# One common set of five PSUM banks for the score and max units, and q and k stored and filled by group of four heads

## The reference

```python
xn = layernorm(x)
# attention
q, k, v = heads(xn @ Wq.T), heads(xn @ Wk.T), heads(xn @ Wv.T)
q, k = rope(q), rope(k)
scores = where(causal, q @ k.T / 4, -1e9)
attn = softmax(scores) @ v
a = merge(attn) @ Wo.T
# feed-forward: a 3-tap mix along the sequence, 9 two-layer paths, one chosen per position
xm = mix(xn)
paths = (xm @ W1[p] + b1[p]) @ W2[p] + b2[p]           # p = 0..8
pick = argmax(tanh(xm @ Wo1 + bo1) @ Wo2 + bo2)
f = layernorm(xn + paths[pick]) * gamma + beta
out = x + a + f
```

## Time and profile before

| | |
|---|---|
| median of 3 runs | 783.06 us |
| the profiled execution | 784.09 us, span of its instructions 782.4 us |
| mean granted TensorE clock | 0.974 |
| PE / DVE / ACT / POOL busy | 739.9 / 641.7 / 448.9 / 288.3 us |
| in 91 to 740 us: PE / DVE / ACT busy | 639.2 / 555.0 / 389.6 of 649 us |

### The profile page before, as it was taken

How to read it: one execution, slowest core, us unless ns; L and a number is a source line. 1 busy time by engine, 2 the same in 40 slices (tenths; PEclk the granted TensorE clock), 3 DMA queues, 4 the chain that set the end, 5 groups by cost and what they waited for, 6 DMA issues and landing times.

```text
span 782.4 us, 12591 instructions
## 1 busy us (share of the span) xinstructions
PE 739.9 (95%) x4416; PEld 372.3 (48%) x4416; DVE 641.7 (82%) x1894; ACT 448.9 (57%) x780; POOL 288.3 (37%) x459
## 2 busy tenths in 40 slices
PE   4869999999999999999999999999999999999996
PEld 2432344354565544345465544445465554354544
DVE  5989999889798789888988789897988669878622
ACT  2262645765655654775656655666657555754672
POOL 2001123990615112893514213695334203130623
PEclk9965999999999999999999999999999999999999
DMA  7259050224613434112651615111560705100103
GB/s 242 97 164 191 8 114 2 72 81 113 105 15 59 105 91 77 53 60 83 118 72 28 136 56 112 33 69 53 122 109 2 136 28 112 33 2 2 28 1 81
DMA packets 40577, 59.98 MB, mean 77 GB/s; under 512 B 4813, under 2 KB 36830, under 8 KB 37634
## 3 DMA queue, kind: packets, MB, share of 16 engines
q1 hardware_dynamic: 36002, 54.39, 29.4%
q0 software_dynamic: 4224, 4.19, 4.1%
q10 hardware_dynamic: 288, 0.59, 0.2%
HBM read 42.04 MB, written 16.85 MB: 75 GB/s over the span
## 4 chain that ended last, share of the span: by engine, by line
PE 71%; POOL 10%; DVE 8%; ACT 6%; DMA 2%; issue 1%; SPq 1%; POOLq 0%; ACTq 0%; DVEq 0%
PE bank L1557 14%; PE bank L1538 14%; PE bank L1519 14%; PE bank L1500 7%; PE bank L1510 6%; PE bank L1462 3%; POOL prob L1014 3%; PE bank L1585 3%; PE bank L1473 3%; ACT prob L1132 3%; POOL raw L993 2%; POOL turned L991 2%; PE bank L1480 2%; PE bank L1567 2%; POOL turned L999 1%
## 5 line engine op out<-in xcount | busy, mean ns | idle before, releaser
L1132 ACT ACTIVATE prob<-bank 128x512 f32<-128x512 f32 x576 | 324.6, 597 | 194.4 <-PE bank L1538 191.3
L1350 DVE CUSTOM_DVE_ANT_0 bank<-bank,causal_sb 128x384 f32<-128x384 f32 (+3 forms) x512 | 240.3, 513 | 34.3 <-PE bank L1519 33.5
L1519 PE MATMUL bank<-k_st,q_st 96*128 96x512 bf16 (+3 forms) x768 | 236.1, 339 | 8.4 <-DMA q_st<-scratch 4.0
L1014 POOL TENSOR_SCALAR_AFFINE_SELECT prob<-prob 128x256 f32<-128x256 f32 (+1 forms) x320 | 125.9, 427 | 294.0 <-ACT prob L1132 291.1
L1538 PE MATMUL bank<-q_st,k_st 98*128 98x512 bf16 (+3 forms) x768 | 212.4, 331 | 7.9 <-ACT prob L1132 5.8
L1353 DVE TENSOR_REDUCE piecemax<-bank 128x1 f32<-128x512 f32 x256 | 164.0, 683 | 18.6 <-PE bank L1519 18.2
L1557 PE MATMUL bank<-prob,v_sb 128*17 128x512 f32 (+3 forms) x1536 | 143.9, 495 | 0.8 <-POOL prob L1014 0.8
L1519 PEld LDWEIGHTS bank<-k_st,q_st 96*128 96x128 bf16 x768 | 72.4, 98 | 130.8 <-DVE piecemax L1350 49.4
L1538 PEld LDWEIGHTS bank<-q_st,k_st 98*128 98x128 bf16 x768 | 70.0, 98 | 113.7 <-ACT prob L1132 56.7
L1510 PE MATMUL bank<-w_sb,mid 128*128 128x256 f32 (+1 forms) x320 | 83.7, 383 | 0.0
L1462 PE MATMUL bank<-xnT,wqk_sb 128*128 128x512 f32 x128 | 68.3, 639 | 4.6 <-ACT xnT L1079 3.7
(11 more groups left out here) (82 smaller groups left out, 698.7 us busy)
## 6 DMA issues: line engine op xcount, KB each, us to landing
scratch<-parts SPq DMA_DIRECT2D x16, 768.0 KB, 3.8
q_st<-scratch SPq DMA_DIRECT2D x90, 128.0 KB, 6.8
k_st<-scratch SPq DMA_DIRECT2D x15, 384.0 KB, 4.6
z<-in_x SPq DMA_DIRECT2D x8, 512.0 KB, 4.5
mask<-chosen SPq DMA_DIRECT2D x16, 256.0 KB
z<-in_x POOLq DMA_DIRECT2D x8, 512.0 KB, 6.7
out<-z SPq DMA_DIRECT2D x8, 512.0 KB, 4.7
k_st<-scratch SPq DMA_DIRECT2D x15, 256.0 KB, 5.4
```

Of the source, the lines that this page charges most:

```text
L1014: nc.gpsimd.affine_select(out=d, in_=d, compare_op=ALU.is_ge, fill=0.0, base=0, pattern=pattern, channel_multiplier=-1).then_inc(masked, 1)
L1132: nc.scalar.activation(prob[:, place_of(G, i), :], ps[:, :], ACT.Exp, scale=float(DK) ** -0.5).then_inc(act_took, 1)
L1350: nc.vector.tensor_tensor_reduce(ps, ps, causal_sb[:, HALF - w:HALF], 1.0, NEG, ALU.add, ALU.max, to).then_inc(dve_took, 1)
L1519: nc.tensor.matmul(begin(("max", G, u))[:, 0:w], q_st[0:PARTS, G % STACKS, h, t * P:(t + 1) * P], k_st[0:PARTS, G % STACKS, h, k0:k0 + w], ...
```

## The change

- Banks: S and max units take their bank from one set of five (1 to 5), the one filled longest ago, whichever kind used it last. The planner is run again with this set, so the whole order after the hand-written part is another one.
- Due times of the max units of groups 2 to 15: from G - 0.95 .. G + 0.03 to G - 1.0 .. G - 0.03. The planner's estimate for a fill goes from 7 to 6 us.
- The rows of the q and k projection are ordered by group, pair and head, so that a group's rows stand on 32 partitions side by side (`GROWS`). The tables of cos and sin follow. The sums stay the same.
- `scratch` is laid out by group, and each store is now four DMAs of 32 partitions, one for each group, 192 KB each. For the first sequence group 0's quarter counts on a semaphore of its own, `first_stored`, and the fill of group 0 waits for that quarter alone. Later fills wait for all quarters.
- `fill` issues the six q DMAs first and waits for k's stores only after them.

```diff
-        a, e = (0, 0.22) if G == 0 else (G - 0.75, G + 0.02) if G == 1 else (G - 0.95, G + 0.03)
+        a, e = (0, 0.22) if G == 0 else (G - 0.75, G + 0.02) if G == 1 else (G - 1.0, G - 0.03)
...
-    return {"S": (1, 2), "max": (3, 4, 5)}.get(what, (6, 7))
+    return (1, 2, 3, 4, 5) if what in ("S", "max") else (6, 7)
...
+        def stores_of(n):
+            return 16 * (NG * (n + 1) - 1)
...
-                eng.dma_start(scratch[n, qk].rearrange("a e p t -> p (a e) t")[:, :, half * HALF:(half + 1) * HALF],
-                              parts[:, i, :, :, :].rearrange("p a e t -> p (a e) t")
-                              ).then_inc(parts_stored[qk][half], 16)
+                for g in range(NG):
+                    done = first_stored[qk][half] if n == 0 and g == 0 else parts_stored[qk][half]
+                    eng.dma_start(scratch[n, qk, g].rearrange("a e p t -> p (a e) t")[:, :, half * HALF:(half + 1) * HALF],
+                                  parts[g * GROWS:(g + 1) * GROWS, i, :, :, :].rearrange("p a e t -> p (a e) t")
+                                  ).then_inc(done, 16)
...
-                for c in (range(half, half + 1) if G == 0 else range(2)):
-                    for qk in range(2):
-                        sp.wait_ge(parts_stored[qk][c], 16 * (n + 1))
+                def stored(qk):
+                    if G == 0:
+                        sp.wait_ge(first_stored[qk][half], 16)
+                    else:
+                        for c in range(2):
+                            sp.wait_ge(parts_stored[qk][c], stores_of(n))
...
+                stored(0)
+                st = q_st[:, G % STACKS, :, a:e]
+                for k, part in enumerate(Q_PARTS):
+                    eng.dma_start(st[k * DK:(k + 1) * DK], src[0][part * DK:(part + 1) * DK]).then_inc(done, 16)
+                stored(1)
                 st = k_st[:, G % STACKS, :, a:e]
                 for row, first, rows in ((0, 0, 3 * DK), (3 * DK, 0, 2 * DK), (5 * DK, 0, DK)):
                     eng.dma_start(st[row:row + rows], src[1][first:first + rows]).then_inc(done, 16)
-                st = q_st[:, G % STACKS, :, a:e]
-                for k, part in enumerate(Q_PARTS):
-                    eng.dma_start(st[k * DK:(k + 1) * DK], src[0][part * DK:(part + 1) * DK]).then_inc(done, 16)
...
-                    act.wait_ge(parts_stored[a][c], 16 * (m + 1))
+                    act.wait_ge(parts_stored[a][c], stores_of(m))
+                    if m == 0:
+                        act.wait_ge(first_stored[a][c], 16)
```

More of the change, by code:

```diff
@@ L29 @@
 HALF = S // 2
+GROWS = P // NG
 HT = NT // 2
@@ L496 @@
           "scale": 1.23, "affine": 1.23, "addx": 0.9}
-DMA_US = {"load": 4.5, "store": 4.0, "fill": 7.0, "keep": 2.5, "spread": 5.0, "place": 2.4, "out": 4.0, "addx": 5.0}
+DMA_US = {"load": 4.5, "store": 4.0, "fill": 6.0, "keep": 2.5, "spread": 5.0, "place": 2.4, "out": 4.0, "addx": 5.0}
 TAKE_US = {"S": 0.5, "shift": 0.48, "v": 0.5, "early": 1.3, "scores": 1.6, "onehot": 0.6, "mid": 0.67,
@@ L804, in build @@
         parts_stored = [[sem(f"parts_stored{a}{c}") for c in range(2)] for a in range(2)]
+        first_stored = [[sem(f"first_stored{a}{c}") for c in range(2)] for a in range(2)]
         stack_filled = [sem(f"stack_filled{k}") for k in range(STACKS)]
@@ L891, in fill @@
                 done = second_filled if half else stack_filled[G % STACKS]
-                src = [scratch[n, qk].rearrange("a e (r h) t -> (a e r) h t", h=H)[:, g * GH:(g + 1) * GH, a:e]
-                       for qk in range(2)]
+                src = [scratch[n, qk, g].rearrange("a e (r h) t -> (a e r) h t", h=GH)[:, :, a:e] for qk in range(2)]
+                stored(0)
[3 more added lines that the diff above has]
+                stored(1)
                 st = k_st[:, G % STACKS, :, a:e]
@@ L1632, in chunks @@
         return w.reshape(w.shape[0] // P, P, w.shape[1]).transpose(1, 0, 2)
-    pair, head = _np.arange(DK // 2)[:, None], _np.arange(H)[None, :]
-    even = (head * DK + 2 * pair).reshape(-1)
+    group, pair, head = _np.meshgrid(_np.arange(NG), _np.arange(DK // 2), _np.arange(GH), indexing="ij")
+    even = ((group * GH + head) * DK + 2 * pair).reshape(-1)
     wqk = _np.concatenate([a["L0_attn_Wq"][even], a["L0_attn_Wq"][even + 1],
@@ L1641 @@
     angle = _np.arange(S, dtype=_np.float32)[:, None] * rates[None, :].astype(_np.float32)
-    cos_t = _np.repeat(_np.cos(angle).T, H, axis=0).astype(_np.float32)
-    sin_t = _np.repeat(_np.sin(angle).T, H, axis=0).astype(_np.float32)
+    cos_t = _np.cos(angle).T[pair.reshape(-1)].astype(_np.float32)
+    sin_t = _np.sin(angle).T[pair.reshape(-1)].astype(_np.float32)
     sent = {
@@ L1671 @@
         args[name] = nc.dram_tensor(f"in_{name}", v.shape, _mybir.dt.from_np(v.dtype), kind="ExternalInput").ap()
-    args["scratch"] = nc.dram_tensor("scratch", (B, 2, 3, 2, P, S), BF16, kind="Internal").ap()
+    args["scratch"] = nc.dram_tensor("scratch", (B, 2, NG, 3, 2, GROWS, S), BF16, kind="Internal").ap()
     args["chosen"] = nc.dram_tensor("chosen", (B, PATHS, S), BF16, kind="Internal").ap()
```

## The result

The changed kernel takes 806.47 us in the median of 4 runs (803.28 to 807.52), the one before 783.63 beside it: a ratio of 1.028, 95% interval 1.024 to 1.032. The profiled execution took 803.28 us, its span 801.6.

A forecast was written before the change was run, and what follows sets the result against it. PE's in-order stream was taken as the bound. 784.09 - 6 + 0 - 1.5 + 1.3 - 1.5 = 776.4 us; with the median 1.03 us below the profiled execution, 775.4, rounded to 775.5; range 767 to 788 us.

The forecast's parts named there:

- What costs nothing: Even part: 48 more store issues on SP (21 us) hidden, places covered by 5.7 us or more of PE work; 0 us.
- Part 3's second term: Start: waiting for the place of group 0's second half, +1.3 us, between 0 and +3; 21 max units charged nothing.
- The clock: Rival, chance 0.08: fuller clock from 57 to 80 us, 771 us; or max run holds it low, +2 to +5.
- Part 3's gain: Start: second fill issued by 50.5, removing DVE's idle 1.49 us; -1.5 us, between 0 and -3.
- slow quarters: Rival, chance 0.10: quarter stores at half of 293 GB/s, second fill 1 to 2 us later; 778 us.
- Part 1: Even part: fewer S units wait for their bank's turn behind ACT; -6 us, bounds 0 and 15 us.
- Part 2: Even part: max units' bank turns, now sharing five banks; 0 us, between -5 us and the first rival's price.
- waits only move: Rival, chance 0.12: PE freed from a bank waits for the next result; Parts 1 and 4 are 0; 783 us.
- Part 4: End: the last group's S units get all five banks; -1.5 us, between 0 and -4.
- The first rival: Chance 0.20: S units wait for banks DVE has not emptied, +12 us, 787.5; sign: tens of S waits for DVE.

The follow-up runs named there:

- bd_start_small: Changed kernel with old rows, stores and fill order, start planned with split banks, seven fills moved behind small transfers on SP; 784.07 us (1.0008).
- after_start_small: Changed kernel with the start planned on split banks and seven fills moved behind small transfers in SP's order; 786.4 us (1.0043).
- before_small_first: Kernel before with seven fills moved behind small transfers in SP's order; 783.67 us (0.9997).
- after_start_split: Changed kernel with the planner on split banks up to its time 1.0, so S units stand between max units in the start; 802.66 us (1.0214).
- d_only: Kernel before with only the new due times of max units and the fill estimate of 6 us; 792.57 us (1.012).
- b_only: Kernel before with only the common set of five banks, which re-plans the order; 789.54 us (1.0085).
- after_place_first: Changed kernel with the second place of seven groups put ahead of the fill in SP's order; 813.87 us (1.0385).

## Why the prediction was wrong

**How far off.** The forecast missed by 31.0 us. 22.4 of them are the three costs above, and 8.6 are the gain that was forecast and that bd_start_small (784.07) does not have.

**The step that failed is "What costs nothing".** It said that the places have 5.7 us or more of PE work between the turning and the S unit that needs them, against 3.4 + 1.7 us. Four things were wrong in it. It asked only about places behind a store, and a store stands ahead of the second place in groups 2, 6 and 10 alone, where nothing waited; in ten other groups it is a fill, or a fill and the output's store, and of fills it said nothing. I took 3.4 us, the place of the start, for the price of every place; behind a fill the landing alone was 10.04 us. I measured the cover from the turning, when what counts is also how long before the place a fill was issued: 2.4 us before, 0.04 us in after for group 3. And I took the second half of a group's S units to begin at unit 12, as my section on the units has it, where it begins at unit 10. So in groups 1, 5, 9 and 13 of the kernel before, the S unit starts only 3.7 to 4.0 us behind the end of the turning; that of group 3 in after came after 10 us, and this was not enough. I had looked at SP's order as a queue of issues, and asked whether an issue is late. It was, by 1.2 to 2.8 us in groups 3, 7 and 11, but the larger part was the transfer. The trace of before already had places that took 6 us behind a fill; I had not looked at their landing. The term was 0, and it measured 15.5 us.

**Part 3's second term, the start.** I took +1.3 us for the place of group 0's second half, and charged nothing for 21 max units in a row, since DVE is busy in either order. The loss there is 10 us in the trace, and 4.6 us are what came back in the time with S units between them. DVE was indeed no busier from 80 to 91 us (10.90 against 10.68), but from 91 to 103 it did 3.4 us less. While PE stands in front of DVE, it does not do the work that needs ACT, and this work is still there when DVE is done. The clock is a rival that no run tests: under "The clock" the prediction had the run of max units hold it low for +2 to +5 us, and from 80 to 103 us it was lower in after, while it is 1.00 throughout in after_start_small. No run changes the order and leaves the clock, so how the 4.6 us divide is open. The other half of that rival, a higher clock from 57 to 80 us, came as well (0.66 against 0.50), but before_small_first, with the order of before, has 0.58 there, so I can't put it down to the change. In after_start_split PE is busy 9.07 of the 11 us from 80 to 91, in place of 6.04:

```profile
80.00:91.00 11.00, 9.07 (x32) 3.22 (x31) 10.70 (x35) 5.71 (x10) 0.00 (x0) 0.84 0.28 86
```

**Part 3's gain.** None. SP in after:

```profile
42.85 5.89 SPq L887 DMA_DIRECT2D scratch<-parts  x8
48.78 4.07 SPq L908 DMA_DIRECT2D q_st<-scratch  x6
52.89 1.88 SPq L912 DMA_DIRECT2D k_st<-scratch  x3
```

I had the stores issued by 46.5 and the second fill by 50.5; they ended at 48.7 and 54.8. I took an issue at 0.43 us from the fills, when the row of the stores themselves gave 0.79 each; measured 0.74. The q fills did follow at once, but k's waited for its quarter, and PE's first max unit on the new half still waited 3.8 us, until 57.3. What I called slow quarters, with 0.10, fits what happened here: 152 GB/s from 57 to 80 us and k's fills at 52.9, though the slower issues alone already put q's at 48.8.

**Part 1 had the size about right, and its gain was spent.** Compare before with after_start_small, which has the common banks and the stores of after, and ends its profile at the same 782.4 us. From 91 to 740 us, summing the time by which each PE unit starts later than the one before it needs, worked out from the starts of matmuls:

```
ahead of            S     max   pv    shift  xnT, paths  all others  sum
before              19.1  19.5  6.1   1.7    0.9         6.1         53.4 us
after_start_small   13.9  17.2  3.9   5.5    5.9         4.3         50.7 us
```

S units lose 5.2 us less, against the 6 forecast, and max units 2.3 less, inside the range of Part 2. Shift units, which wait for DVE's cut, lose 3.8 us more, and `xnT` and `paths` 5.0 more. These hang on the price given to each matmul: with other prices the same starts give 4.4 and 2.1 us for S and max, and nothing net. The 2.7 us are not in the time either, since bd_start_small, with the same order and the old stores, stands at 784.07 against 784.02. So the S units waited less, and PE waited elsewhere. The "waits only move" rival, which I gave 0.12, is what the common banks by themselves come to. In the waits of after_start_small S units stand 86 times behind ACT and 35 times behind DVE, 121 in all, where they stood 139 times behind ACT:

```profile
PEld bank L1542 <- DVE piecemax L1373: 36.0, 92, 1.7
PEld bank L1561 <- ACT prob L1155: 28.4, 86, 1.0
PEld bank L1542 <- DVE piecemax L1376: 21.9, 57, 0.9
...
PEld bank L1561 <- DVE piecemax L1373: 14.1, 27, 1.5
...
PEld bank L1561 <- DVE piecemax L1376: 3.2, 8, 0.6
```

**Part 4** had the right sign: from the start of the last max unit to that of the last projection 43.7 us before, 43.2 after, 0.5 us won against 1.5 forecast. Half a microsecond is within what two executions differ by.

**The first rival.** Its sign appeared, 41 waits of S units for DVE in after, but I had said that only it could lengthen the even part. A transfer could too. The range of 767 to 788 us was built from PSUM and clock alone, and held nothing for a queue that I had declared covered.

**Still open:** why d_only costs 9 us. Its trace has three waits of 2.1 to 2.3 us of `pv` for POOL's masking (167.9, 350.1 and 534.2 us), behind `rope` on POOL, and the rest in pieces; no run takes these away. The same goes for b_only's wait for DVE. No run sends the places from another queue than the fills, which would tell the order within a queue from the load on the DMA engines. And 2.3 us between after_start_small and bd_start_small is from medians; the spans of the two profiles differ by 0.6.

## What to carry to other kernels

A transfer's time is not its size's: ask of every small one that something waits for what was issued on the same queue in the 10 us before it, and when a change moves either, measure the cover from the large one. When a change lets the order run one kind of unit for long, ask what the other engines have to do meanwhile; equal busy time of the slowest engine is not equal time. And when a bank constraint is loosened, compare at the same order and at the new one: here each order was good only with the banks that it was planned for, and the freedom was worth nothing in the one order that was planned for it.

## What the runs showed of the hardware

- A 4 KB transfer, issued right behind nine that carry 1.5 MB on SP's queue, landed after 10.04 us, and 512 KB in the same position after 9.62 us, against 1.69 and 3.0 us elsewhere. In the kernel before, 2.4 us behind such a fill, it took 6.0 us. The Trainium skill (DMA: Bandwidth & Descriptors, Queues, rings and completion order) says that SP owns one ring on each DMA engine, whose descriptors are consumed in order; the trace agrees in that the place lands 0.3 us behind the fill's last transfer (228.29 and 228.03), and seven fills moved behind the small ones were worth 15.5 us.
- Stores split into four of 32 partitions cost 2.6 us of the kernel's time (interval 0.5 to 3.4), split into three of 128 nothing, with 64 and 48 issues in place of 16. In the 6 us from 43 us on they moved 176 and 250 GB/s, the full width 228 and 293. SP took 0.72 to 0.74 us for each of the first, 0.58 for each of the second.
- VectorE's operations on 4 elements, 0.15 us in the rows beside them, took 1.16 and 1.20 us while GpSimd ran passes of 1.27 us.
- Within waits of TensorE of 7.23 and 8.83 us (after_place_first) the granted clock fell to the lower level and was 0.50 for some 10 us. Behind those of 2.47 and 2.61 us (after) it was 0.50 from 230 to 233 and from 602 to 605 us. A short stretch of this kind also stands in the kernel before, where PE is busy all of the time from 278 to 285 us and the clock is 0.57 from 281 on, so a short one is not put down to a wait for certain.
